# Cross-attention on one core: scores in units that run across tiles, with eight halved slots

## The chip, the cores and the metric

The kernel runs on 1 core of one Trainium2 chip. The metric is the device time of one execution in microseconds (us); the number given for a kernel is the median of its runs.

## The reference

Cross-attention with 16 heads of 32 columns, computed for batch 0 alone. Its result, 512 rows of 512 columns, is added to each of the 32 batches of `x`.

```python
q, k, v = tgt @ Wq.T, memory @ Wk.T, memory @ Wv.T   # then split in 16 heads of 32
scores = einsum('bhqd,bhkd->bhqk', q, k) / sqrt(32)
att = einsum('bhqk,bhkd->bhqd', softmax(scores), v)
return tgt + att[0]          # tgt is x, (32, 512, 512) float32; memory is ctx_1024
```

So the arithmetic is that of one batch, and the traffic is `x` in and out: 2 x 33.6 MB, and 4 MB of weights and context.

## The kernel before, in words

Rows. A row of `x` belongs to a partition p, a half J (0 or 1) and a place r (0 or 1) in it: the rearrangement is `b (j p r) d -> p j b r d`. Tile j of the attention (128 rows) is half j // 2, place j % 2. A *slot* in SBUF holds one half of two batches (1 MiB: 4 KB on a partition for each batch). There are 18 slots and 16 groups of two batches (`GROUPS`), so half 0 of all groups and groups 0 and 1 of half 1 fit; the other 14 groups of half 1 are loaded into slots after their rows of half 0 have been stored. In the first part slots 8 to 17 hold weights and context, raw and turned, and are loaded with `x` once those are dead.

Units of adding. When the attention of heads 0 to 7 of tile 0 is there, `FIRST` adds it to the left half of the columns of the *halved* slots (`HALVED`); `SECOND` adds heads 8 to 15 to their right half, and the whole row to the other slots. `ROW_1` is tile 1, `ROW_2` and `ROW_3` are tiles 2 and 3, in half 1. POOL and DVE share the additions by lists of groups (`POOL_HALVED`, `DVE_HALVED`, `POOL_WHOLE`, `DVE_WHOLE`, `POOL_GROUPS`, `DVE_GROUPS`).

DMA. Everything is issued by SP, on one queue, in an order written out by hand (L234 to L280): weights and loads, FIRST's stores, SECOND's stores, with reloads of the first rows of half 1 (`reload_row(0, g)`, for the groups of `BY_ROWS`) behind them, then ROW_1's stores, each followed by a reload that waits for a store three slots back, then the stores of half 1 (`STORED_BY_ROWS` first, row by row, then `LAST_STORE_ORDER`). Where SP waits for an addition, all that stands behind it in this order waits too. A row of a halved slot's store is 1 KB long, that of a whole row 2 KB, and loads or stores of both rows have 4 KB.

Compute. PE multiplies scores (`scores`: three passes of high and low parts, a head's 32 rows being a quarter of the array), DVE takes each head's negative maximum (`head_max`, L684), ACT the exponential and its sum (`exponent`, L604), PE turns the probabilities (`turn_probs`, L405), ACT copies them out (`copy_transposed`, L612), PE weighs the values of four heads (`weigh_values`, L416), DVE copies that out (`copy_att_t`, L696), PE turns it back (`turn_back`, L428), and DVE multiplies with the inverse sums (`normalize`, L710 and L712). Scores have four PSUM banks, head h in bank h % 4, so a head's scores wait for the exponential four heads back. Between the heads of tile j PE makes tile j + 1's queries (`query_chunk`, L347) and turns them (`turn_queries`); ACT empties both. All engines follow orders written out by hand: `heads(j)` on PE, ACT and DVE for tiles 1 to 3, and explicit lists for tile 0. In `heads` before, a tile's first four heads are scored as a group during the tile before, the other twelve in six pairs (`score_pair`).

Of the kernel before, what the change touches and what calls it, by code (L numbers as in the profile page):

```python
# [12 lines left out]
HEADS = 16  # L13
# [6 lines left out]
def cross_attention_add(nc, x, ctx, wq, wk, wv, out):  # L20
# [12 lines left out]
    PAIR = 2  # L33
    PAIRS = HEADS // PAIR
# [24 lines left out]
    LAST_STORE_ORDER = (6, 7, 8, 1, 2, 3, 4, 5, 0, 9, 10, 11, 12, 13, 14, 15)  # L59

    FIRST_ORDER = (0, 1, 3, 2, 5, 7, 4, 6, 9, 8, 10, 11)
    SECOND_ORDER = (0, 1, 2, 3, 4, 5, 6, 7, 8, 9, 10, 11, 12, 14, 13, 15)
# [5 lines left out]
    with ExitStack() as stack:  # L68
# [47 lines left out]
        stored = [sem(f"stored{g}") for g in range(GROUPS)]  # L116
        ident_ready = sem("ident_ready")
# [47 lines left out]
        def scores_through(j, h):  # L165

            if j == 0:  # L170
                return h // HPG + 1
            return HG + (j - 1) * (PAIRS - 1) + (1 if h < HPG else h // PAIR)

# [19 lines left out]
        def _(sp):  # L193
# [48 lines left out]
            for g in range(1, GROUPS):  # L242
# [17 lines left out]
            for n, g in enumerate(SECOND_ORDER):  # L260
# [55 lines left out]
        def _(pe):  # L316
# [53 lines left out]
            def value_chunk(t, c):  # L370
# [7 lines left out]
                if c == C - 1:  # L378
                    last.then_inc(bank_filled, 1)

# [8 lines left out]
            def score_group(j, g):  # L389
                if j == 0:  # L390
                    emptied(pe, "k_t", g)
                if j * HG + g > 0:
                    pe.wait_ge(exp_ready, j * HEADS + g * HPG)
                scores(j, range(g * HPG, (g + 1) * HPG))

            def score_pair(j, pair):
                pe.wait_ge(exp_ready, j * HEADS + pair * PAIR - PAIR)
                scores(j, range(pair * PAIR, (pair + 1) * PAIR))

# [32 lines left out]
            def heads(j):  # L432
# [4 lines left out]
                score_pair(j, 2)  # L437
# [6 lines left out]
                score_pair(j, 3)  # L444
                turn_probs(j, 4)
                turn_probs(j, 5)
# [3 lines left out]
                score_pair(j, 4)  # L450
                turn_probs(j, 6)
                if more:
                    pe.wait_ge(att_t_ready, j * HG + 1)
                    query_chunk(j + 1, 0)
                turn_probs(j, 7)
                if more:
                    query_chunk(j + 1, 1)
                score_pair(j, 5)
                turn_probs(j, 8)
                if more:  # L460
                    query_chunk(j + 1, 2)
                turn_probs(j, 9)
                if more:
                    query_chunk(j + 1, 3)
                score_pair(j, 6)
# [3 lines left out]
                turn_probs(j, 10)  # L469
                if more:  # L470
                    pe.wait_ge(att_t_ready, j * HG + 2)
                    turn_queries(j + 1)
                turn_probs(j, 11)
                score_pair(j, 7)
# [4 lines left out]
                weigh_values(j, 2)  # L479
                turn_probs(j, 14)  # L480
                turn_probs(j, 15)
                if more:
                    score_group(j + 1, 0)
# [51 lines left out]
            score_group(0, 0)  # L535
# [9 lines left out]
            score_group(0, 1)  # L545
# [44 lines left out]
        def _(act):  # L590
# [24 lines left out]
            def heads(j):  # L615
                for h in range(HEADS):
# [28 lines left out]
            exponent(0, 8)  # L645
            exponent(0, 9)
            copy_transposed(0, 6)
            copy_transposed(0, 7)
            exponent(0, 10)
            empty("q", 1)  # L650
# [3 lines left out]
            copy_transposed(0, 10)  # L654
            empty("q_t", 1)
            exponent(0, 12)
            copy_transposed(0, 11)
            exponent(0, 13)
            copy_transposed(0, 12)
# [9 lines left out]
        def _(dve):  # L669
# [71 lines left out]
            def heads(j, unit, adds):  # L741

                for h in range(HPG, HEADS):
                    if h % HPG == 0 and h >= 2 * HPG:
                        copy_att_t(j, h // HPG - 2)
                    if h == HEADS - 2 and j + 1 < T:
                        empty("q_t", j + 1)  # L750
                    head_max(j, h)
                    if h % HPG == 2 and h > HPG:
                        invert_sums(j, h // HPG - 1)
# [84 lines left out]
```

## Time and profile before

| | |
|---|---|
| median of 3 runs | 188.89 us (188.24 to 189.64) |
| the profiled execution | 189.16 us, of which the span (first to last instruction) is 187.1 |
| busy: PE, DVE, ACT, POOL | 130.9, 100.8, 96.7, 80.3 us |
| DMA | 71.52 MB, on the average 382 GB/s; HBM read 37.75 MB, written 33.55 MB |
| granted TensorE clock | 0.893 on the average: full until the last matmul, half after it |

Busy time is no limit by itself here: an engine's order and its waits decide when a unit's sums exist, and SP's queue decides when they can leave. A stretch of the trace is best read by its GB/s and then by what SP waited for.

### The profile page before, as it was taken

How to read it: one execution, taken by the hardware profiler on the slowest of the kernel's cores; microseconds unless marked ns; L12 is line 12 of the kernel's file. 1: busy time of each engine (PE TensorE's matmuls, PEld its weight loads, DVE VectorE, ACT ScalarE, POOL GpSimd, SP SyncE). 2: the span in 40 equal slices, each digit the busy share in tenths (PEclk: the TensorE clock that was granted, in tenths of full speed). 3: DMA queues.
4: the chain of work that ended last, by engine and by line, in shares of the span. 5: the costliest groups of instructions: out<-in, count | busy, mean ns of one | idle time of the engine just before them, and what ended most of it. 6: DMA issues, size and time to landing. Idle time of an engine off the chain costs nothing.

```text
span 187.1 us, 3330 instructions
## 1 busy us (share of the span) xinstructions
PE 130.9 (70%) x1224; PEld 92.0 (49%) x1224; DVE 100.8 (54%) x161; ACT 96.7 (52%) x225; POOL 80.3 (43%) x43
## 2 busy tenths in 40 slices
PE   6999999999996887998979998889884000000000
PEld 6978857677654665556656556656653000000000
DVE  0263226625517889927399659665453999800000
ACT  2344536378266979777789569698892000000000
POOL 1000000000006959950059999089992999700000
PEclk9999999999999999999999999999999755555555
DMA  6999999999999989999999999999999999999994
GB/s 200 369 384 420 409 408 411 409 409 408 349 404 403 342 294 316 340 299 398 405 387 399 355 401 407 407 403 409 412 416 412 405 421 416 408 421 421 421 421 172
DMA packets 30880, 71.52 MB, mean 382 GB/s; under 512 B 1808, under 2 KB 7952, under 8 KB 30736
## 3 DMA queue, kind: packets, MB, share of 16 engines
q1 hardware_dynamic: 30864, 71.31, 99.7%
q8 instruction: 10, 0.16, 0.3%
q14 instruction: 6, 0.05, 0.1%
HBM read 37.75 MB, written 33.55 MB: 381 GB/s over the span
## 4 chain that ended last, share of the span: by engine, by line
PE 54%; ACT 15%; DVE 11%; issue 6%; DVEq 1%; POOL 0%; ACTq 0%; POOLq 0%
PE bank L405 12%; PE bank L385 8%; ACT probs L604 8%; PE bank L347 8%; PE bank L365 6%; PE bank L376 6%; ACT probs_t L612 5%; PE bank L340 5%; DVE slots L738 5%; PE bank L416 4%; DVE slots L728 3%; PE bank L488 3%; DVE neg_max L684 2%; PE bank L428 1%; DVEq L68 1%
## 5 line engine op out<-in xcount | busy, mean ns | idle before, releaser
L295 POOL TENSOR_TENSOR slots<-slots,att_rows 128x512 f32<-128x512 f32 (+1 forms) x25 | 43.0, 1765 | 72.4 <-DVE att_rows L710 72.4
L604 ACT ACTIVATE probs<-bank,neg_max 128x512 f32<-128x512 f32 x64 | 44.8, 702 | 11.6 <-DVE neg_max L684 11.2
L684 DVE TENSOR_REDUCE neg_max<-bank 128x1 f32<-128x512 f32 x64 | 41.7, 681 | 13.6 <-PE bank L385 13.4
L405 PE MATMUL bank<-ident,probs 128*128 128x128 f32 x256 | 39.8, 281 | 7.7 <-ACT probs L604 6.7
L612 ACT COPY probs_t<-bank 128x512 f32<-128x512 f32 x64 | 37.6, 591 | 11.5 <-PE bank L405 10.5
L405 PEld LDWEIGHTS bank<-ident,probs 128*128 128x128 f32 x256 | 28.1, 141 | 23.3 <-ACT probs L604 17.7
L385 PE MATMUL bank<-k_t,q_t 32*128 32x512 f32 x192 | 24.1, 425 | 0.0
L304 POOL TENSOR_TENSOR slots<-slots,att_rows 128x1024 f32<-128x1024 f32 x8 | 18.6, 2360 | 5.6 <-DVE att_rows L710 5.6
L312 POOL TENSOR_TENSOR slots<-slots,att_rows 128x2048 f32<-128x2048 f32 x4 | 18.0, 4522 | 3.4 <-DVE att_rows L710 3.4
L416 PE MATMUL bank<-probs_t,v 128*32 128x128 f32 x512 | 17.3, 276 | 0.7 <-ACT probs_t L612 0.7
L721 DVE TENSOR_TENSOR slots<-slots,bank 128x512 f32<-128x512 f32 (+1 forms) x19 | 17.5, 930 | 0.1
L347 PE MATMUL bank<-wq_t,att_rows 128*128 128x512 f32 x32 | 16.3, 600 | 0.0
L385 PEld LDWEIGHTS bank<-k_t,q_t 32*128 32x128 f32 x192 | 12.2, 183 | 7.9 <-issue 3.8
L416 PEld LDWEIGHTS bank<-probs_t,v 128*32 128x32 f32 x512 | 13.0, 110 | 5.8 <-issue 2.7
L696 DVE COPY att_t<-bank 128x128 f32<-128x128 f32 x16 | 4.5, 284 | 18.3 <-PE bank L416 18.3
L365 PE MATMUL bank<-ctx_t,wk_t 128*128 128x512 f32 x48 | 13.3, 409 | 0.4 <-ACT ctx_t L598 0.3
L604 ACT ACTIVATION_READ_ACCUMULATOR probs<-bank,neg_max 128x1 f32 x64 | 13.6, 212 | 0.0
L376 PE MATMUL bank<-wv_t,ctx_t 128*128 128x512 f32 x48 | 13.3, 410 | 0.0
L365 PEld LDWEIGHTS bank<-ctx_t,wk_t 128*128 128x128 f32 x48 | 8.3, 189 | 2.3 <-ACT ctx_t L598 0.6
L376 PEld LDWEIGHTS bank<-wv_t,ctx_t 128*128 128x128 f32 x48 | 8.3, 189 | 2.0 <-issue 0.7
L728 DVE TENSOR_TENSOR slots<-slots,bank 128x1024 f32<-128x1024 f32 x8 | 9.1, 1214 | 0.0
L738 DVE TENSOR_TENSOR slots<-slots,bank 128x2048 f32<-128x2048 f32 x4 | 8.9, 2277 | 0.0
(41 smaller groups left out, 91.3 us busy)
## 6 DMA issues: line engine op xcount, KB each, us to landing
slots<-in_x_dram SPq DMA_DIRECT2D x21, 1024.0 KB, 15.6
out_dram<-slots SPq DMA_DIRECT2D x30, 512.0 KB, 9.8
slots<-in_x_dram SPq DMA_DIRECT2D x22, 512.0 KB, 8.9
out_dram<-slots SPq DMA_DIRECT2D x11, 1024.0 KB, 13.5
out_dram<-slots SPq DMA_DIRECT2D x24, 256.0 KB, 3.3
ctx_raw<-in_ctx_dram SPq DMA_DIRECT2D x1, 1024.0 KB, 5.0
wq_raw<-in_L_xattn_Wq_dram SPq DMA_DIRECT2D x1, 1024.0 KB, 9.2
wv_raw<-in_L_xattn_Wv_dram SPq DMA_DIRECT2D x1, 1024.0 KB, 12.1
```

Source lines behind the costliest of these rows:

```text
L295: nc.gpsimd.tensor_tensor(xs, xs, a.unsqueeze(1).to_broadcast([P, BPS, a.shape[1]]), ALU.add).then_inc(added[g], 1)
L304: nc.gpsimd.tensor_tensor(xs, xs, att.unsqueeze(1).to_broadcast([P, BPS, D]), ALU.add).then_inc(row_2_added[g], 1)
L347: last = mm(job_bank("q", j), x0_t[:, c, :], wq_t[:, c, :], start=(c == 0), stop=(c == C - 1))
L365: last = mm(job_bank("k_t", g), wk_t[:, c, a, g * P:(g + 1) * P], ctx_t[:, c, b, :], start=(c == 0 and (a, b) == PASSES[0]), stop=(c == C ...
L376: last = mm(job_bank("v", t), ctx_t[:, c, a, t * P:(t + 1) * P], wv_t[:, c, b, :], start=(c == 0 and (a, b) == PASSES[0]), stop=(c == C - ...
L385: last = mm(bank[:, h % S_BANKS, :], q_t[rows, j % 2, g, a, :], k_t[rows, g, b, :], start=((a, b) == PASSES[0]), stop=((a, b) == PASSES[-1]))
L405: last = nc.tensor.transpose(bank[:, PT_BANK + h % 2, t * P:(t + 1) * P], probs[:, h % 2, t * P:(t + 1) * P], ident[:, :])
L416: last = mm(att_t_ps[i * DK:(i + 1) * DK, g, :], v[:, t, h * DK:(h + 1) * DK], probs_t[:, (j * HEADS + h) % PT_SLOTS, t, :], start=(t == 0 ...
L604: nc.scalar.activation(probs[:, h % 2, :], bank[:, h % S_BANKS, :], ACT.Exp, bias=neg_max[:, h:h + 1], scale=1.0, accum_out=row_sum[:, h:h ...
L612: nc.scalar.copy(probs_t[:, (j * HEADS + h) % PT_SLOTS, :, :], bank[:, PT_BANK + h % 2, :].rearrange("p (t n) -> p t n", t=T)).then_inc(pr ...
L684: nc.vector.tensor_reduce(neg_max[:, h:h + 1], bank[:, h % S_BANKS, :], AX_X, ALU.max, negate=True).then_inc(max_ready, 1)
L738: nc.vector.tensor_tensor(xs, xs, back.unsqueeze(1).to_broadcast([P, BPS, ROWS * D]), ALU.add).then_inc(added[g], 1)
```

## The change

- Tiles 1 to 3 are scored in six *units* of heads (0-2, 3-5, 6-8, 9-11, 12-13, 14-15) instead of a group of four and six pairs. Unit 0 of the next tile is scored before turns 14 and 15 and weighing 3, not between turn 15 and weighing 3.
- DVE takes the maxima of a unit together, and an addition or other work between units (`heads` on DVE). Of the next tile it takes heads 0 to 2 ahead of the tile's end.
- In tile 0, PE weighs heads 0 to 7 and scores heads 12 to 15 earlier; the queries of tile 1 come out later (two after the last scores); ACT and DVE follow in their lists.
- Eight slots are halved instead of twelve; `BY_ROWS` has 7 groups instead of 10, `STORED_BY_ROWS` 3 instead of 5, `ROW_LAG` is 12 instead of 13, and the orders of stores follow.
- Slots 14 and 16, which hold the first halves of `ctx_t` and `wv_t`, are loaded after half of the last value tile's chunks (`half_values_done`), slots 15 and 17 after all of them as before.

```diff
+    UNITS = (range(0, 3), range(3, 6), range(6, 9), range(9, 12), range(12, 14), range(14, 16))
-    HALVED = range(12)
-    POOL_HALVED, DVE_HALVED = (1, 3, 5, 7, 9, 10, 11), (0, 2, 4, 6, 8)
-    POOL_WHOLE, DVE_WHOLE = (13, 15), (12, 14)
+    HALVED = range(8)
+    POOL_HALVED, DVE_HALVED = (1, 3, 5, 7), (0, 2, 4, 6)
+    POOL_WHOLE, DVE_WHOLE = (9, 11, 13, 15), (8, 10, 12, 14)
-    BY_ROWS = range(FRESH, FRESH + 10)
-    ADDED_BY_ROWS, STORED_BY_ROWS = (1, 2, 3, 4, 5, 6, 7, 8), (1, 2, 3, 4, 5)
-    LAST_ROW_DVE_GROUPS = (6, 7, 8, 1, 2, 3, 4, 5)
+    BY_ROWS = range(FRESH, FRESH + 7)
+    ADDED_BY_ROWS, STORED_BY_ROWS = (1, 2, 3, 4, 5, 6, 7, 8), (1, 2, 3)
+    LAST_ROW_DVE_GROUPS = (4, 5, 6, 7, 8, 1, 2, 3)
...
-                if g == CTX_T:
-                    sp.wait_ge(bank_filled, number["v", T - 1] + 1)
-                load(0, g)
-            for g in range(FRESH):
-                load(LAST_HALF, g)
-
-            LAG, ROW_LAG = 3, 13
+                if g < CTX_T:
+                    load(0, g)
+            sp.wait_ge(half_values_done, 1)
+            load(0, CTX_T)
+            load(LAST_HALF, 0)
+            sp.wait_ge(bank_filled, number["v", T - 1] + 1)
+            load(0, CTX_T + 1)
+            load(LAST_HALF, 1)
+
+            LAG, ROW_LAG = 3, 12
...
+            def score_unit(j, u):
+
+                pe.wait_ge(exp_ready, j * HEADS + UNITS[u].stop - S_BANKS)
+                scores(j, UNITS[u])
...
                 turn_probs(j, 13)
                 if more:
                     emptied(pe, "q_t", j + 1)
                 weigh_values(j, 2)
+                if more:
+                    score_unit(j + 1, 0)
                 turn_probs(j, 14)
                 turn_probs(j, 15)
-                if more:
-                    score_group(j + 1, 0)
                 weigh_values(j, 3)
...
-            score_group(0, 2)
-            query_chunk(1, 0)
+            score_group(2)
             emptied(pe, "v", T - 1)
             weigh_values(0, 0)
+            query_chunk(1, 0)
+            turn_probs(0, 8)
             query_chunk(1, 1)
-            turn_probs(0, 8)
-            query_chunk(1, 2)
             turn_probs(0, 9)
-            query_chunk(1, 3)
             weigh_values(0, 1)
             turn_probs(0, 10)
+            score_group(3)
+            turn_probs(0, 11)
+            query_chunk(1, 2)
+            query_chunk(1, 3)
+            turn_probs(0, 12)
             raw_queries_out(1)
             turn_back(0, range(HG // 2))
-            turn_probs(0, 11)
-            score_group(0, 3)
             turn_queries(1)
-            turn_probs(0, 12)
             turn_probs(0, 13)
+            turn_probs(0, 14)
             emptied(pe, "q_t", 1)
+            score_unit(1, 0)
             weigh_values(0, 2)
-            turn_probs(0, 14)
             turn_probs(0, 15)
-            score_group(1, 0)
             weigh_values(0, 3)
...
             copy_transposed(0, 10)
+            copy_transposed(0, 11)
+            exponent(0, 12)
+            exponent(0, 13)
+            empty("q", 1)
+            copy_transposed(0, 12)
             empty("q_t", 1)
...
+                maxima(1)
+                next_add()
+                maxima(2)
+                invert_sums(j, 0)
+                copy_att_t(j, 0)
+                next_add()
+                maxima(3)
+                invert_sums(j, 1)
+                next_add()
+                maxima(4)
+                copy_att_t(j, 1)
+                next_add()
+                maxima(5)
                 if j + 1 < T:
-                    head_max(j + 1, 0)
-                    head_max(j + 1, 1)
-                copy_att_t(j, HG - 1)
+                    empty("q_t", j + 1)
+                invert_sums(j, 2)
+                next_add()
+                copy_att_t(j, 2)
                 if j + 1 < T:
-                    head_max(j + 1, 2)
-                    head_max(j + 1, 3)
+                    for h in UNITS[0]:
+                        head_max(j + 1, h)
+                next_add()
+                invert_sums(j, 3)
+                copy_att_t(j, 3)
...
             normalize(SECOND, slice(HEADS // 2, HEADS))
             add(SECOND, DVE_HALVED[0])
-            head_max(1, 3)
-            add(SECOND, DVE_HALVED[1])
-            heads(1, SECOND, list(DVE_HALVED[2:] + DVE_WHOLE))
+            head_max(1, 2)
+            for g in DVE_HALVED[1:]:
+                add(SECOND, g)
+            heads(1, SECOND, list(DVE_WHOLE))
```

On PE, `heads` has its units between the same turns in the order: turns 0, 1, unit 1, turns 2, 3, unit 2, turn 4, weighing 0, turn 5, query 0, turn 6, query 1, unit 3, turn 7, query 2, turn 8, query 3, unit 4, turn 9, weighing 1, turn 10, unit 5, turn 11, the turned queries, turns 12, 13, weighing 2, the next tile's unit 0, turns 14, 15, weighing 3. On ACT, the raw queries of the next tile are emptied after exponential 9 instead of 10, the turned ones after 12 instead of 11.

## Rows read from the trace of the kernel before

**Rows 1.** The page's slices: DMA share in tenths and GB/s, 40 slices.

```profile
DMA  6999999999999989999999999999999999999994
GB/s 200 369 384 420 409 408 411 409 409 408 349 404 403 342 294 316 340 299 398 405 387 399 355 401 407 407 403 409 412 416 412 405 421 416 408 421 421 421 421 172
```

**Rows 2.** Stretches: busy us of each engine, clock, DMA share, GB/s.

```profile
48.00:52.00 4.00, 4.00 (x53) 2.23 (x51) 3.17 (x6) 1.76 (x5) 0.00 (x0) 1.00 0.94 338
...
68.00:72.00 4.00, 3.08 (x24) 2.21 (x23) 3.97 (x9) 3.52 (x10) 3.35 (x3) 1.00 0.76 253
74.00:80.00 6.00, 5.84 (x60) 3.67 (x60) 5.13 (x9) 4.97 (x14) 6.00 (x5) 1.00 1.02 344
...
81.00:86.00 5.00, 5.00 (x55) 3.05 (x54) 1.67 (x6) 3.46 (x8) 0.97 (x1) 1.00 1.02 315
...
97.70:187.10 89.40, 41.00 (x470) 27.07 (x470) 48.18 (x67) 36.53 (x90) 55.74 (x21) 0.78 1.01 396
...
110.00:130.00 20.00, 18.13 (x234) 12.60 (x230) 13.64 (x26) 16.17 (x41) 14.41 (x7) 1.00 1.05 406
...
164.00:182.00 18.00, 0.00 (x0) 0.00 (x0) 0.00 (x0) 0.00 (x0) 0.00 (x0) 0.50 1.03 422
```

**Rows 3.** SP's issues in time; single stores with time from issue to landing.

```profile
58.83 20.75 SPq L201 DMA_DIRECT2D out_dram<-slots  x26
...
146.34 2.61 SPq L207 DMA_DIRECT2D out_dram<-slots  x3
...
L201 SPq DMA_DIRECT2D out_dram<-slots x1: 373/373/373, 69.7 to 69.7; - x1
...
DMA to landing us min/median/max: 2.5/2.5/2.5
...
L201 SPq DMA_DIRECT2D out_dram<-slots x1: 383/383/383, 97.7 to 97.7; - x1
...
DMA to landing us min/median/max: 5.1/5.1/5.1
```

**Rows 4.** The chain that ended last: start, us on the chain, what.

```profile
34.05 0.90 PE bank L385 x12
...
74.82 1.01 PE bank L416 x32
75.83 0.90 PE bank L385 x6
76.73 0.59 PE bank L405 x4
77.32 0.86 PE bank L347 x2
78.18 0.44 PE bank L405 x4
```

**Rows 5.** ACT in time: start, us, line, operation, idle before it.

```profile
62.50 0.73 ACT L604 ACTIVATE probs<-bank,neg_max 128x512 f32<-128x512 f32 x1
63.08 0.24 ACT L604 ACTIVATION_READ_ACCUMULATOR probs<-bank,neg_max 128x1 f32 x1
63.17 0.62 ACT L612 COPY probs_t<-bank 128x512 f32<-128x512 f32 x1
...
71.01 0.69 ACT L604 ACTIVATE probs<-bank,neg_max 128x512 f32<-128x512 f32 x1
```

**Rows 6.** DVE and POOL in time: maxima and sums.

```profile
49.52 2.48 DVE L684 TENSOR_REDUCE neg_max<-bank 128x1 f32<-128x512 f32 x4 [0.66 <-PE bank L385]
...
68.94 0.69 DVE L721 TENSOR_TENSOR slots<-slots,bank 128x512 f32<-128x512 f32 x1
...
75.30 1.21 DVE L721 TENSOR_TENSOR slots<-slots,bank 128x1024 f32<-128x1024 f32 x1
...
96.44 1.22 DVE L721 TENSOR_TENSOR slots<-slots,bank 128x1024 f32<-128x1024 f32 x1
...
68.65 13.32 POOL L295 TENSOR_TENSOR slots<-slots,att_rows 128x512 f32<-128x512 f32 x9 [2.13 <-DVE att_rows L710]
```

More of the change, by code:

```diff
@@ L171, in scores_through @@
                 return h // HPG + 1
-            return HG + (j - 1) * (PAIRS - 1) + (1 if h < HPG else h // PAIR)
+            return HG + (j - 1) * len(UNITS) + 1 + [h in unit for unit in UNITS].index(True)
         def slot_of(J, g):
@@ L250, in _ @@
                     sp.wait_ge(bank_filled, number["k_t", HG - 1] + 1)
[L251 to L257 removed]
+                if g < CTX_T:
[7 more added lines that the diff above has]
+            LAG, ROW_LAG = 3, 12
             for g in FIRST_ORDER:
                 store(FIRST, g)
[L260 removed]
+            for n, g in enumerate(range(GROUPS)):
                 store(SECOND, g)
@@ L379, in value_chunk @@
                     last.then_inc(bank_filled, 1)
+                if (t, c) == (T - 1, C // 2 - 1):
+                    last.then_inc(half_values_done, 1)
             def scores(j, heads_at_once):
@@ L387, in scores, with score_group @@
                 last.then_inc(scores_ready, 1)
[L389 to L398, printed above, removed]
+            def score_group(g):
+                emptied(pe, "k_t", g)
+                if g > 0:
+                    pe.wait_ge(exp_ready, g * HPG)
+                scores(0, range(g * HPG, (g + 1) * HPG))
+            def score_unit(j, u):
+                pe.wait_ge(exp_ready, j * HEADS + UNITS[u].stop - S_BANKS)
+                scores(j, UNITS[u])
             def turn_probs(j, h):
@@ L454, in heads @@
                     query_chunk(j + 1, 0)
+                turn_probs(j, 6)
+                if more:
+                    query_chunk(j + 1, 1)
+                score_unit(j, 3)
                 turn_probs(j, 7)
                 if more:
-                    query_chunk(j + 1, 1)
-                score_pair(j, 5)
+                    query_chunk(j + 1, 2)
                 turn_probs(j, 8)
                 if more:
-                    query_chunk(j + 1, 2)
+                    query_chunk(j + 1, 3)
+                score_unit(j, 4)
                 turn_probs(j, 9)
-                if more:
-                    query_chunk(j + 1, 3)
-                score_pair(j, 6)
                 if more:
@@ L469, in heads @@
                 turn_probs(j, 10)
+                score_unit(j, 5)
+                turn_probs(j, 11)
                 if more:
@@ L479, in heads @@
                 weigh_values(j, 2)
+                if more:
+                    score_unit(j + 1, 0)
                 turn_probs(j, 14)
                 turn_probs(j, 15)
-                if more:
-                    score_group(j + 1, 0)
                 weigh_values(j, 3)
@@ L741, in heads, with maxima, next_add @@
             def heads(j, unit, adds):
[L746 to L753, printed above, removed]
-                    if adds and (h % 2 == 1 or cols_of(unit, adds[0]) != slice(0, D)):
-                        add(unit, adds.pop(0))
-                copy_att_t(j, HG - 2)
-                invert_sums(j, HG - 1)
+                def maxima(u):
+                    for h in UNITS[u]:
+                        head_max(j, h)
+                def next_add():
+                    if adds:
+                        add(unit, adds.pop(0))
+                maxima(1)
[11 more added lines that the diff above has]
+                maxima(5)
                 if j + 1 < T:
-                    head_max(j + 1, 0)
-                    head_max(j + 1, 1)
-                copy_att_t(j, HG - 1)
+                    empty("q_t", j + 1)
+                invert_sums(j, 2)
+                next_add()
+                copy_att_t(j, 2)
                 if j + 1 < T:
-                    head_max(j + 1, 2)
-                    head_max(j + 1, 3)
+                    for h in UNITS[0]:
[3 more added lines that the diff above has]
+                copy_att_t(j, 3)
             for what, i, _ in JOBS[:number["wv_t", C - 1] + 1]:
@@ L776, in _ @@
             empty("v", 3)
-            for h in range(2 * HPG, 3 * HPG):
-                head_max(0, h)
+            head_max(0, 8)
+            head_max(0, 9)
             invert_sums(0, 0)
             copy_att_t(0, 0)
+            head_max(0, 10)
+            head_max(0, 11)
             invert_sums(0, 1)
             copy_att_t(0, 1)
+            for h in range(3 * HPG, HEADS):
+                head_max(0, h)
             normalize(FIRST, slice(0, HEADS // 2))
             add(FIRST, DVE_HALVED[0])
-            head_max(0, 12)
-            head_max(0, 13)
+            empty("q_t", 1)
             add(FIRST, DVE_HALVED[1])
-            head_max(0, 14)
-            empty("q_t", 1)
-            head_max(0, 15)
-            for g in DVE_HALVED[2:]:
-                add(FIRST, g)
+            add(FIRST, DVE_HALVED[2])
             invert_sums(0, 2)
+            head_max(1, 0)
             copy_att_t(0, 2)
+            add(FIRST, DVE_HALVED[3])
+            head_max(1, 1)
             invert_sums(0, 3)
-            head_max(1, 0)
-            head_max(1, 1)
             copy_att_t(0, 3)
-            head_max(1, 2)
             normalize(SECOND, slice(HEADS // 2, HEADS))
             add(SECOND, DVE_HALVED[0])
-            head_max(1, 3)
-            add(SECOND, DVE_HALVED[1])
-            heads(1, SECOND, list(DVE_HALVED[2:] + DVE_WHOLE))
+            head_max(1, 2)
+            for g in DVE_HALVED[1:]:
+                add(SECOND, g)
+            heads(1, SECOND, list(DVE_WHOLE))
             normalize(ROW_1, before=SECOND)
```

33 lines of the change are left out of this document (11 added, 22 removed).

## Prediction

> **What bounds the kernel now.** I read the page's slices first: the DMA share stands at 9 tenths or more from the second slice to the last but one, with one 8, and GB/s is about 400 except in two hollows [rows 1]. The engines are not like that: from 164 to 182 none of them is busy at all [rows 2], and the span ends at 187.1 with transfers alone. So the kernel is a stream of 71.5 MB on one in-order queue, SP's, and an engine counts only where SP has nothing left to issue.
>
> The stretches give the prices [rows 2]: 406 GB/s in runs of 2 KB (110 to 130), 422 GB/s in runs of 4 KB (164 to 182), 344 GB/s in the 1 KB runs of halved stores (74 to 80). Two stretches lose time because the queue is dry: 48 to 52 (338 GB/s; SP waits for the last values before it loads slots 14 to 17) and 68 to 72 (253 GB/s; the twelve FIRST stores are through, SECOND's first sum comes at 69.6). Then SP's issues [rows 3]: FIRST's stores go out from 58.83, ROW_1's from 97.7. SECOND's first store, issued at 69.7 into a dry queue, landed 2.5 us later; ROW_1's first, issued at 97.7, took 5.1. It is 256 KB larger, 0.6 us at 406 GB/s, so on a dry queue it would have landed after 3.1: 2.0 us of other transfers still lay ahead. ROW_1 today arrives with 2.0 us to spare.
>
> **The change part by part.**
>
> *Traffic.* Total bytes stay. Eight halved slots instead of twelve turn 2.1 MB from 1 KB into 2 KB runs: 6.1 - 5.2 = 0.9 us less. Slots 9 to 11 are no longer reloaded row by row. So SP has 7 row reloads (3.7 MB) instead of 10 to send after SECOND, and after ROW_1's first store 36.2 MB remain instead of 34.6: three row loads fewer (-1.57 MB at 406: -3.9 us), three whole ones more (3.15 MB at 422: +7.5), two slots stored whole instead of in rows (-0.2): **+3.4 us** of work behind ROW_1. As a check, 97.7 to 187.1 at 396 GB/s is 35.4 MB [rows 2]: those 34.6 and 0.8 of backlog, the 2.0 us above.
>
> The Trainium skill ("DMA: Bandwidth & Descriptors", Specifications) puts a core's limit to HBM at about 358 GB/s; by it every such difference would cost about an eighth more (estimate from that page: the 3.4 would be 3.9). The trace runs at 406 to 422 [rows 2] and disagrees; the sum goes by the rows.
>
> *Loads 14 and 16 half a value tile earlier.* That fills the hollow at 48 to 52 (4 us at 338 instead of 406: 0.7 us). It only helps if FIRST follows without a gap.
>
> *Tile 0.* I walk PE, ACT and DVE in their new order with the durations of [rows 4, 5]: weighing 1.0, scores 0.9, turned head 0.44 to 0.59, query pair of matmuls 0.86, exponential 0.67 of ACT's time (0.82 until its sum is read), copy 0.6 until done (ACT goes on 0.47 after its start), maximum 0.60 apart [rows 6], under 0.1 for each hand-over. The start is the third score group, the same in both (its maxima begin at 49.52 [rows 6], PE is free at 49.4). Weighing 0, queries 0 and 1 around turn 8, turn 9 at 52.75 (after copy 7), weighing 1 to 54.35, turn 10, scores of 12 to 15 at 54.9, turn 11, queries 2 and 3 to 58.05. ACT now takes exponentials 12 and 13 ahead of the raw queries, which it empties at 58.35 to 58.95; the turn back waits for them, and so FIRST is multiplied at 59.4 and its first sum done at 60.9. **FIRST's first store goes out at 60.95 instead of 58.83.** The wait that caused it is the one for the raw queries; behind it on PE stand the turned queries and turns 13 and 14. Then: turned queries 59.25, exponential 14 at 60.4, turn 14 at 61.25, unit 0 of tile 1 at 61.85, weighing 2 at 62.75, turn 15 at 63.75, copies 14 and 15, weighing 3 at 65.15, copied out at 66.3, turned back 66.65, multiplied 67.1, SECOND's first sum from 67.9 instead of 68.94: **1.0 earlier**.
>
> *Tile 1.* PE loses one of seven score stages: pairs and groups of four both take 0.90 [rows 4], so units of three are costed at 0.90 too (bounds 0.90 and 1.35, by heads; nearest to both rows). That is 0.9 us less PE work. But DVE now runs SECOND's sum 0, the maximum of head 2 and three more sums (0.6 each) before the maximum of head 3, which comes at 70.9; exponential 3 starts at 71.6, against 71.01 [rows 5]. Unit 2 needs exponential 4 (73.6), weighing 0 is at 75.1, its copy on DVE behind three maxima at 76.5, the first query at 76.85. From there PE has 11.2 us without a gap to 88.0 (four queries, units 3 to 5, turns 6 to 12, weighing 1, turned queries). It then waits for exponential 13, which stands on ACT behind the turned queries' copy, till 89.1. Turn 13, weighing 2, next tile's unit 0, turns 14 and 15 follow; weighing 3 must wait for copy 15, which the next tile's scores no longer cover, till 93.5. Copied out 94.65, turned back 95.0, multiplied 95.7, ROW_1's first sum from 97.0 instead of 96.44 [rows 6]. What the units save on PE goes into these two waits. **ROW_1's first store: 98.25 instead of 97.7.**
>
> *SECOND's whole sums.* DVE's slots 8, 10, 12, 14 now each follow a unit's maxima. Number 12 follows unit 3 (scored 79.05, maxima to 81.9): done 83.1 instead of 76.5 [rows 6]. POOL's nine sums now take 13.3, to 82.0 [rows 6]; three halved ones go and two whole ones come, each worth about two halved, and it starts a microsecond earlier: done at 81 to 83 again, and slot 13 is in time. SP issues in slot order, so behind slot 12's store stand three more stores and seven reloads.
>
> **The sum.** The queue after FIRST: loads end at 60 to 61, dry till 62.8 (60.95 and 1.85, the 2.5 of [rows 3] less its 0.65 of transfer), eight stores of 0.76 to 68.9, dry till 70.4, SECOND's first twelve slots to about 82, dry till 85.0 when slot 12 comes (83.15 and 1.85), then eleven transfers of 1.29: 99.2, or 100.3 with the 1.1 us that the turn from stores to loads costs now (81 to 86 at 315 GB/s [rows 2]). ROW_1's first store adds 1.85 to 98.25: 100.1. So two gates, the late sum and the late ROW_1, close at the same time. ROW_1's store lands at 98.25 + 3.1 = 101.4 on a dry queue, against 102.8 now: -1.4. Work behind it: +3.4. Slot 2's sum waits for three maxima of tile 2 (about 101.1) and leaves 0.4 dry. Sum **+2.4 us**: 189.16 + 2.4 = 191.6 for the profiled execution, 188.89 + 2.4 = **191.3** for the median. The 2.1 us between execution and span stay. Costs bounded from both sides: units at 1.35 add up to 2.3 us in tile 1 (five units) before PE's waits take some; the hand-overs, 0 to 0.1 for some thirty steps, are worth 1.5 either way; so 189.8 to 193.6 for this case alone. The last tile is no gate: from 100.1 the queue has 18.5 MiB of ROW_1's stores and reloads and three row stores ahead of the first whole slot, to about 152; now that slot's store goes out at 146.34 [rows 3], so tiles 2 and 3 would have to take 3 us longer than today to be late.
>
> **The rivals.**
> (a) *Faster: the queue never dries behind FIRST.* If SECOND's sum 0 were ready by 67 and slot 12 and ROW_1 kept ahead, the stream alone would count: 62.8 + 6.1 (FIRST) + 6.1 and 10.3 (SECOND's halves and whole rows) + 9.0 (seven reloads) + 1.1 (the turn) = 95.4 for ROW_1, 4.7 before the forecast: 186.6. It decides if ROW_1's first store is issued before 93.7, 4 us earlier than now. For it: one score stage less. Against it: PE's waits are for ACT. Chance 0.13.
> (b) *No change: the units do shorten tile 1 by 2 to 3 us* (exponential 13 and copy 15 not waited for: 1.1 + 0.9, and sum 12 as much earlier). ROW_1's stream begins at 97 to 98: 188.3 to 189.5. For it: ACT and PE both stand idle at those two places, so a small shift in order closes them. Chance 0.26.
> (c) *The added sums between units hold up ROW_1's and SECOND's stores as well*, a dry microsecond at each of slots 4, 6 and 8: 194 to 195. Chance 0.07.
> (d) *The forecast:* 0.54.
>
> **How the numbers follow.** One per cent, 1.9 us, is what a measurement here can tell from no change. Range 187.2 to 193.8: it leaves out (a) and (c), 0.2 together. Faster by over 1% (under 187.0): 0.11 of (a) and 0.03 of (b)'s lower edge, 0.14. Slower by over 1% (over 190.8): most of (d), 0.46, and all of (c), 0.07, together 0.53. Within: 0.33.
>
> **What would show it.** Right: FIRST's first store near 61, hollows in GB/s near 61 and 83, ROW_1's first store after 97 and landing about 3 us later, slot 12's sum after 82. Wrong: ROW_1's first store before 95 with transfers queued ahead of it, or PE without gaps after turn 12. A unit of three that takes over 1.0 would be a price of mine that fell.

## The result, and the profile after

The changed kernel takes 193.55 us (median of four runs, 193.23 to 193.69) beside 188.56 us of the kernel before in the same runs (188.03 to 189.64): ratio 1.0255, 95% interval 1.0204 to 1.0305. It is slower, as forecast, and inside the range; the size is +5.0 us where +2.4 was forecast. The profiled execution took 193.44 us, its span 191.7, so 1.7 lies outside it (2.1 before). Ratios here and below leave out executions more than 1.5% above the fastest of the same kernel (among them two of four in e3 and in e4, four of ten in e8 and in e10; the profiles of e3 and e8 are of such executions and are not used), so a ratio can differ from that of two medians.

The page's slices of after (TensorE clock in tenths, DMA share in tenths, GB/s; a slice is 4.8 us):

```profile
PEclk9999999999999996999999999999999855555555
DMA  6999999999997979649999999999999999999995
GB/s 214 365 373 421 408 409 409 409 409 410 410 405 283 337 253 362 242 150 355 403 399 361 282 401 400 404 417 418 410 412 419 407 421 421 412 419 420 423 421 233
```

The hollow of before in slice 11 [rows 1] is filled, and new ones stand in slices 13, 15, 17 and 18: 283, 253, 242, 150. The clock's line has a 6 at slice 16, which before had nowhere until its last matmul. The stretches of after say when and why (busy us of each engine, clock, DMA share, GB/s):

```profile
46.85:58.00 11.15, 10.69 (x122) 6.40 (x120) 6.29 (x13) 7.83 (x20) 0.00 (x0) 1.00 1.03 409
60.00:62.00 2.00, 1.82 (x25) 1.26 (x29) 2.00 (x5) 1.28 (x5) 2.00 (x3) 1.00 0.65 229
66.00:68.00 2.00, 2.00 (x20) 1.43 (x19) 1.97 (x5) 0.58 (x1) 1.53 (x2) 1.00 0.56 187
73.00:76.00 3.00, 3.00 (x34) 1.93 (x34) 1.97 (x4) 1.73 (x5) 3.00 (x2) 0.50 1.04 362
78.00:80.00 2.00, 2.00 (x16) 1.08 (x14) 0.06 (x1) 1.72 (x5) 2.00 (x2) 1.00 0.51 187
82.00:84.00 2.00, 2.00 (x11) 0.82 (x10) 1.44 (x3) 1.69 (x5) 0.00 (x0) 1.00 0.04 11
84.00:86.00 2.00, 2.00 (x40) 1.55 (x40) 1.66 (x4) 1.63 (x5) 0.00 (x0) 1.00 0.84 261
86.00:88.00 2.00, 2.00 (x17) 1.51 (x16) 1.96 (x3) 1.59 (x4) 0.00 (x0) 1.00 0.99 275
88.00:98.00 10.00, 7.89 (x114) 5.79 (x113) 5.68 (x12) 7.73 (x20) 1.24 (x1) 1.00 1.05 400
98.57:191.70 93.13, 39.30 (x472) 26.20 (x470) 48.93 (x68) 37.60 (x91) 55.71 (x21) 0.78 1.01 395
150.00:186.00 36.00, 0.00 (x0) 0.00 (x0) 16.49 (x11) 0.00 (x0) 15.99 (x4) 0.52 1.03 418
```

A low GB/s with a share near 1 is slow transfers; a low share is a queue with nothing to send, called dry here. A *gate* is a store that SP cannot issue before its sum exists, while all that stands behind it in SP's order waits too. At 82 to 84 the share is 0.04, and SP waits for slot 12's sum. SP's issues, its waits for these sums of DVE (37.7 us in 13 waits, the longest 12.1; before, 20.0 us in 8), and ROW_1's first store from issue to landing:

```profile
59.93 23.91 SPq L198 DMA_DIRECT2D out_dram<-slots  x21
...
98.57 3.84 SPq L198 DMA_DIRECT2D out_dram<-slots  x4
...
SPq L198 <- DVE slots L723: 37.7, 13, 12.1
...
L198 SPq DMA_DIRECT2D out_dram<-slots x1: 384/384/384, 98.6 to 98.6; - x1
...
DMA to landing us min/median/max: 5.2/5.2/5.2
```

ROW_1's first store was issued at 98.57, 0.9 later than before [rows 3], and landed at 98.57 + 5.2 = 103.8. The sum turned on this number: 101.4 was forecast, 102.8 was before. From it to the span's end are 191.7 - 103.8 = 87.9 us, against 187.1 - 102.8 = 84.3 before: +3.6, where +3.4 was forecast.

PE in time (start, us, line, operation, idle before it and its cause), then DVE:

```profile
71.31 0.66 PE L408 MATMUL bank<-ident,probs 128*128 128x128 f32 x4 [1.73 <-ACT probs L606]
72.47 1.29 PE L387 MATMUL bank<-k_t,q_t 32*128 32x512 f32 x9 [0.50 <-ACT probs L606]
73.68 1.12 PE L408 MATMUL bank<-ident,probs 128*128 128x128 f32 x4
74.73 1.84 PE L419 MATMUL bank<-probs_t,v 128*32 128x128 f32 x32
...
79.34 0.97 PE L387 MATMUL bank<-k_t,q_t 32*128 32x512 f32 x9
...
84.48 1.08 PE L419 MATMUL bank<-probs_t,v 128*32 128x128 f32 x32
...
89.48 0.66 PE L408 MATMUL bank<-ident,probs 128*128 128x128 f32 x4 [0.97 <-ACT probs L606]
...
93.80 1.08 PE L419 MATMUL bank<-probs_t,v 128*32 128x128 f32 x32 [0.73 <-ACT probs_t L614]
```

```profile
58.42 0.42 DVE L712 TENSOR_TENSOR att_rows<-bank,recip 128x256 f32<-128x256 f32 x1 [1.04 <-PE bank L431]
...
66.77 0.69 DVE L723 TENSOR_TENSOR slots<-slots,bank 128x512 f32<-128x512 f32 x1
...
82.25 1.19 DVE L723 TENSOR_TENSOR slots<-slots,bank 128x1024 f32<-128x1024 f32 x1
...
95.99 0.69 DVE L712 TENSOR_TENSOR att_rows<-bank,recip 128x512 f32<-128x512 f32 x1 [0.75 <-PE bank L431]
...
97.32 1.22 DVE L723 TENSOR_TENSOR slots<-slots,bank 128x1024 f32<-128x1024 f32 x1
...
123.50 0.69 DVE L712 TENSOR_TENSOR att_rows<-bank,recip 128x512 f32<-128x512 f32 x1 [0.75 <-PE bank L431]
...
147.23 0.69 DVE L712 TENSOR_TENSOR att_rows<-bank,recip 128x512 f32<-128x512 f32 x1 [0.75 <-PE bank L431]
```

Nine matmuls are a unit of three: 0.97 to its last end, 0.90 to the start of the next (79.34, then 80.25), the price forecast; the two waits for ACT (0.97 and 0.73) are the forecast's 1.1 and 0.9. Not forecast is the half clock from 73 to 76, after PE had idled 1.73: there a unit takes 1.29 and a weighing 1.84 instead of 1.08.

### The profile page after: what moved, and what is told of

Its sections match the earlier page's. It is cut to its first block and busy times, and to the rows that moved or that the text cites. A ratio compares the mean times of both kernels' runs of the same rounds, so it can differ in the third digit from the quotient of the medians.

```text
span 191.7 us, 3318 instructions
## 1 busy us (share of the span) xinstructions
PE 128.3 (67%) x1224; PEld 90.6 (47%) x1224; DVE 102.5 (53%) x161; ACT 97.4 (51%) x225; POOL 77.4 (40%) x39
## 5 line engine op out<-in xcount | busy, mean ns | idle before, releaser
L295 POOL TENSOR_TENSOR slots<-slots,att_rows 128x1024 f32<-128x1024 f32 (+1 forms) x21 | 40.1, 1945 | 76.1 <-DVE att_rows L712 76.1
L686 DVE TENSOR_REDUCE neg_max<-bank 128x1 f32<-128x512 f32 x64 | 40.5, 684 | 19.4 <-PE bank L387 19.3
L387 PE MATMUL bank<-k_t,q_t 32*128 32x512 f32 x192 | 21.6, 431 | 3.3 <-ACT probs L606 3.3
L419 PE MATMUL bank<-probs_t,v 128*32 128x128 f32 x512 | 18.1, 284 | 2.8 <-ACT probs_t L614 2.8
L723 DVE TENSOR_TENSOR slots<-slots,bank 128x1024 f32<-128x1024 f32 (+1 forms) x19 | 18.5, 984 | 0.1
L419 PEld LDWEIGHTS bank<-probs_t,v 128*32 128x32 f32 x512 | 13.6, 113 | 6.4 <-ACT probs_t L614 3.9
L387 PEld LDWEIGHTS bank<-k_t,q_t 32*128 32x128 f32 x192 | 10.8, 183 | 10.9 <-ACT probs L606 6.5
```

The lines of the kernel that those rows point to most:

```text
L295: nc.gpsimd.tensor_tensor(xs, xs, a.unsqueeze(1).to_broadcast([P, BPS, a.shape[1]]), ALU.add).then_inc(added[g], 1)
L387: last = mm(bank[:, h % S_BANKS, :], q_t[rows, j % 2, g, a, :], k_t[rows, g, b, :], start=((a, b) == PASSES[0]), stop=((a, b) == PASSES[-1]))
L419: last = mm(att_t_ps[i * DK:(i + 1) * DK, g, :], v[:, t, h * DK:(h + 1) * DK], probs_t[:, (j * HEADS + h) % PT_SLOTS, t, :], start=(t == 0 ...
L686: nc.vector.tensor_reduce(neg_max[:, h:h + 1], bank[:, h % S_BANKS, :], AX_X, ALU.max, negate=True).then_inc(max_ready, 1)
L723: nc.vector.tensor_tensor(xs, xs, a.unsqueeze(1).to_broadcast([P, BPS, a.shape[1]]), ALU.add).then_inc(added[g], 1)
```

## The experiments

Two theories stood at first. Q: the queue decides, by the time that it is dry ahead of ROW_1's stores and the work that is left behind them. R: the work behind ROW_1 alone (three groups fewer by rows) is the loss. Where an expectation names another rival, the run's reading says what it is.

**e1: ten groups by rows again.** Diff against after:

```diff
-    BY_ROWS = range(FRESH, FRESH + 7)
+    BY_ROWS = range(FRESH, FRESH + 10)
```

> The changed kernel with 10 groups in BY_ROWS again instead of 7 and nothing else: three more row loads go out between SECOND's stores and ROW_1's, and 3.4 us less work is left behind ROW_1. Theory Q (two gates on one queue: slot 12's late sum, with everything behind it, binds first): the three loads stand behind slot 12 in either place, so no change, 193.0 to 194.0. Rival R (what counts is how much is left behind ROW_1): 3.4 us faster, 190.1. Rival C (tile 1's arithmetic is slower, the queue only follows): no change.

Measured 193.85 us, ratio 1.0254 (1.0163 to 1.0345). No gain; R falls. The work behind ROW_1's store did shrink, to 84.15 us, but the store itself was issued at 99.25 and landed 8.7 later:

```profile
L198 SPq DMA_DIRECT2D out_dram<-slots x1: 383/383/383, 99.2 to 99.2; - x1
...
DMA to landing us min/median/max: 8.7/8.7/8.7
```

```profile
82.00:84.00 2.00, 2.00 (x10) 0.93 (x9) 2.00 (x4) 1.69 (x5) 0.00 (x0) 1.00 0.04 8
```

The three added row reloads stood behind slot 12's store, and the dry stretch ahead of that stayed. So bytes moved from behind one gate to in front of it shortened nothing here, where they filled no dry stretch.

**e2: reloads from the tenth store on,** ahead of the late sum.

```diff
-            LAG, ROW_LAG = 3, 12
+            LAG, ROW_LAG = 3, 9
```

> The changed kernel with ROW_LAG 9 instead of 12: the seven row loads go out behind SECOND's stores of slots 9 to 15, so three of them lie ahead of the wait for slot 12's sum and fill the dry stretches at 78 to 80 and 82 to 85. Q: the first gate opens 2.6 to 3.9 us earlier, then ROW_1's own first store (issued 98.6, 1.85 to the first byte, against 101.7 now) binds: 1.0 to 1.5 us faster, 192.0 to 192.5. R: no change, the bytes behind ROW_1 are the same. C: no change.

Measured 194.88 us, 1.0287 (1.0224 to 1.0351), no gain where Q had 1 to 1.5. Stretches:

```profile
78.00:88.00 10.00, 10.00 (x83) 6.02 (x85) 6.69 (x11) 7.26 (x17) 3.64 (x2) 0.98 0.96 322
88.00:90.00 2.00, 1.98 (x18) 1.37 (x14) 1.80 (x3) 1.77 (x5) 0.00 (x0) 1.00 0.87 145
98.00:102.00 4.00, 2.74 (x24) 1.82 (x22) 3.97 (x7) 3.57 (x9) 3.78 (x2) 1.00 0.44 163
```

The hollow at 78 to 88 is mostly filled, and the queue is dry at 98 to 102 instead, for ROW_1 (issued at 100.03, landed 2.8 later). Two gates stood one behind the other. This profile also has half a clock from 72 to 78, 3.4 us longer than after, and ROW_1's store goes out 1.5 later; the execution whose mean clock was nearest to after's (0.887, after 0.886) took 193.32, no gain that shows either.

**e3: both,** `BY_ROWS` of ten and `ROW_LAG` 8.

> Both edits, 10 groups in BY_ROWS and ROW_LAG 8. Q: the gate of slot 12 opens and 3.4 us of work leave the place behind ROW_1, so the gains no longer hide each other: 1.3 + 3.4 = 4.7 us faster, 188.5 to 189.5, though the two alone give 0 and 1.3. R: 3.4 faster, 190.1, as with the ten groups alone. C: no change.

Measured 1.013 (1.0062 to 1.0197), from two of four executions (191.56 and 191.62; the others took 194.82 and 195.12). In these two both edits together give some 2 us of the 4.7 expected, where neither gave anything alone; the interval overlaps that of e1, so this is a sign and not settled.

**e4: DVE takes each of the maxima 3, 4, 5 of tile 1 ahead of one of SECOND's halved sums** (`first=2` leaves that unit out of `heads`).

```diff
...
-            for g in DVE_HALVED[1:]:
+            for h, g in zip(UNITS[1], DVE_HALVED[1:]):
+                head_max(1, h)
                 add(SECOND, g)
-            heads(1, SECOND, list(DVE_WHOLE))
+            heads(1, SECOND, list(DVE_WHOLE), first=2)
```

> The changed kernel with DVE's order at the start of tile 1 changed: maxima of heads 3, 4, 5 each ahead of one of SECOND's sums 2, 4, 6 instead of behind all three; all on SP as in the changed kernel. Exponential 3 should start about 0.8 us earlier (69.7 instead of 70.5), and if the granted clock no longer falls at 72.5 to 76.5 another 1.5 us come back. Q: slot 12's sum and ROW_1 move together, 0.8 to 2.3 us faster, 191.2 to 192.7. R: no change. C: the same 0.8 to 2.3, so this run tells only R from the others and shows whether the clock's fall hangs on PE's idle time before turn 3.

Ratio 1.0157 (1.0084 to 1.023), from two of four executions, 191.74 and 192.47, in the range of Q and C; the others took 196.09 and 197.03. In the profiled one, 191.74, PE's idle time before turn 3 fell from 1.73 to 0.98, the clock stayed full, ROW_1's first store landed at 97.24 + 4.9 = 102.1. By this DVE's order at that place is worth about 1% (1.0255 less 1.0157), but the two intervals overlap, and the same edit gains nothing that shows in e10.

**e5: PE kept busy in that gap** by twelve turns of the identity into an unused bank, which change no result.

```diff
                 turn_probs(j, 2)
+                if j == 1:
+                    pe.wait_ge(probs_t_ready, j * HEADS + 2)
+                    for _ in range(12):
+                        nc.tensor.transpose(bank[:, PT_BANK + 1, 0:P], ident[:, :], ident[:, :])
                 turn_probs(j, 3)
```

> The changed kernel with twelve transposes of the identity (overwritten by the next turn) between turns 2 and 3 of tile 1, where PE otherwise idles for 1.73 us; nothing else is moved. Theory K (the fall of the granted clock behind that idle time costs what tile 1 loses): the clock stays at full through 72 to 76, slot 12's sum and ROW_1 come 1.2 to 1.5 us earlier, 192.0 to 192.5 against 193.5. Rival S (the clock falls for another reason, or the stretch at half the clock is hidden): no change in the clock or none in the time, 193.2 to 193.8.

Measured 193.62 us, 1.0234 (1.0199 to 1.0269): no gain that shows, in the range of S. Its stretches:

```profile
72.00:76.00 4.00, 3.50 (x53) 2.25 (x50) 3.29 (x8) 3.22 (x9) 4.00 (x2) 1.00 1.02 353
...
100.00:105.00 5.00, 4.76 (x50) 3.46 (x51) 3.31 (x7) 2.68 (x9) 5.00 (x3) 0.66 1.01 363
```

The clock held at 72 to 76, slot 12's sum came 22.53 us behind FIRST's multiplication (58.80 to 81.33) instead of 23.83 (58.42 to 82.25), and ROW_1's store landed at 102.1, as in e4. Then the clock fell in tile 2, after 1.27 of idle, and once more at 128, and 89.3 us lay behind that store instead of 87.9. So K had the clock and the sums right and the time wrong. The fall at 73 is worth 1.3 us at ROW_1; that it costs the kernel that much is not shown: of e5's four executions the one with the highest mean clock, 0.893, took 193.79, the two with the lowest, 0.880, 193.23 and 193.45.

**e6: the change's compute with the slots of before** (twelve halved, ten by rows, `ROW_LAG` 13 and the store orders of before). **e7: the reverse,** compute of before with the change's slots and loads as before. The lines of the slots are those of the diff of the change.

> All of the changed kernel's order of compute on PE, ACT and DVE, with the slots, shares and store orders of the kernel before (twelve halved, ten reloaded by rows). Q (the queue: eight halved slots put 3.4 us behind ROW_1 and leave two dry stretches in SECOND): most of the loss goes, only ROW_1 comes about 1 us later than before, 189.5 to 190.5. C (the loss is in the new order of compute): stays at 193 to 194.

> The kernel before, its order of compute untouched, with the changed kernel's slots (eight halved, seven reloaded by rows, lag 12, store orders). Q: FIRST's eight stores end at 67, dry until SECOND at 71.4, ROW_1's store on an almost empty queue at 99.5 and 3.4 us more behind it: 191.0 to 192.0. C: as the kernel before, 188.5 to 189.3.

e6 192.02 us, 1.0151 (1.0092 to 1.0209); e7 191.77 us, 1.0134 (1.0098 to 1.0171). e7 is in Q's range; e6 is over Q's and under C's, so both rivals missed there. Each half of the change costs by itself, and their sum, 1.0285, is about the whole, 1.0255. In e7 the stretches that SECOND's and slot 10's sums leave dry:

```profile
66.00:70.00 4.00, 3.26 (x25) 2.40 (x24) 3.97 (x9) 3.52 (x10) 2.44 (x2) 1.00 0.15 50
...
78.00:80.00 2.00, 2.00 (x10) 0.91 (x10) 1.65 (x2) 1.97 (x5) 2.00 (x2) 1.00 0.29 103
```

FIRST now has eight stores instead of twelve, four times 0.76 us less to send before SECOND is there; the whole sums that took the place come later than halved ones did.

**e8: e1, e4 and `ROW_LAG` 8 together.**

> The changed kernel with ten groups by rows, lag 8 and the maxima of heads 3 to 5 each ahead of one of SECOND's sums. Q: slot 12 is no gate, 3.4 us less stand behind ROW_1, and ROW_1's first store goes out at about 97.2 as in the run with the maxima first: 188 to 189, the kernel before within a per cent. C: only the maxima's gain, 191.5.

Ten executions, median 192.23 (189.86 to 194.56); the ratio, 1.0082 (1.0037 to 1.0127), is that of the faster six. 188 to 189 was expected, and the best four were at 189.86 to 190.02. In those most of the loss is taken back; a gain over before was not reached.

**e9: tile 0's new order and the split loads alone,** with pairs, `heads` and slots of before. **e11: the split loads alone,** added to before.

```diff
-                if g == CTX_T:
-                    sp.wait_ge(bank_filled, number["v", T - 1] + 1)
-                load(0, g)
-            for g in range(FRESH):
-                load(LAST_HALF, g)
+                if g < CTX_T:
+                    load(0, g)
+            sp.wait_ge(half_values_done, 1)
+            load(0, CTX_T)
+            load(LAST_HALF, 0)
+            sp.wait_ge(bank_filled, number["v", T - 1] + 1)
+            load(0, CTX_T + 1)
+            load(LAST_HALF, 1)
...
```

> Tile 0's new order and the split loads of the change alone: tiles 1 to 3 with the group and six pairs of the kernel before, twelve halved slots and its store orders. Q (the queue; what moves is when SECOND and ROW_1 reach it): SECOND about 2 us earlier, FIRST's twelve stores run into it without a dry stretch, tile 1 as long as before, so ROW_1's first store goes out about 1.5 us earlier and still meets a backlog; the two hollows of before close: 0.8 to 1.5 us faster than before, 187.5 to 188.3. Rival T (tile 0's order is what costs, since FIRST comes 2 us later): 1 to 2 us slower than before.

> The kernel before with slots 14 and 16 loaded after half of the last value tile's chunks, and nothing else. The hollow at 48 to 52 closes. Q: FIRST's first store then finds the queue almost empty and the dry time before SECOND grows by what was won; ROW_1 still meets a smaller backlog: 0 to 0.5 us faster, 188.6 to 189.2 beside 189.2. Rival L (loads set the pace): 0.7 faster.

e9 189.86 us (median of twelve), 1.0058 (1.0024 to 1.0091): slower by a little, where Q had it faster, though ROW_1 is earlier. Its multiplications of ROW_1 to ROW_3, SP's issues and a stretch:

```profile
93.28 0.68 DVE L717 TENSOR_TENSOR att_rows<-bank,recip 128x512 f32<-128x512 f32 x1
...
119.86 0.68 DVE L717 TENSOR_TENSOR att_rows<-bank,recip 128x512 f32<-128x512 f32 x1
...
141.88 0.69 DVE L717 TENSOR_TENSOR att_rows<-bank,recip 128x512 f32<-128x512 f32 x1 [0.75 <-PE bank L435]
```

```profile
60.85 20.79 SPq L203 DMA_DIRECT2D out_dram<-slots  x26
...
95.85 3.28 SPq L203 DMA_DIRECT2D out_dram<-slots  x4
```

```profile
60.00:62.00 2.00, 1.08 (x18) 0.74 (x20) 1.97 (x5) 2.00 (x6) 2.00 (x2) 1.00 0.20 74
```

ROW_1's store is issued at 95.85 and lands 8.1 later, at 104.0: the queue, not ROW_1, holds it. FIRST's first store, at 60.85 as the forecast had it (60.95), found that queue dry: at 74 instead of 408 GB/s the stretch 60 to 62 loses 1.6 us, about what the kernel lost (1.1 by the ratio). So T, that FIRST's delay costs by itself, is borne out. e11 measured 188.74 us, 1.0017 (0.9989 to 1.0045): filling the hollow at 48 to 52 alone gains nothing that shows.

**e10: e6 with e4's order of maxima.**

> The changed kernel's compute with the slots of the kernel before (as the run with twelve halved), and the maxima of heads 3 to 5 each ahead of one of SECOND's sums. Q, with the start of tile 1 as the place where the new order loses: PE's idle time before turn 3 falls from 2.3 us to about 1.0, ROW_1's first store from 99.9 to 97.5, and the time to that of before within 1 us, 188.5 to 189.8. U (the units themselves lengthen tile 1): stays near 192.

Ten executions, median 192.02 (190.10 to 193.50), 1.0124 (1.0082 to 1.0166) by the faster six; 188.5 to 189.8 was expected, and it is not told apart from e6, whose interval overlaps.

**e12: before with split loads, fourteen halved slots and twelve groups by rows,** the slots moved the other way.

```diff
-    HALVED = range(12)
-    POOL_HALVED, DVE_HALVED = (1, 3, 5, 7, 9, 10, 11), (0, 2, 4, 6, 8)
-    POOL_WHOLE, DVE_WHOLE = (13, 15), (12, 14)
+    HALVED = range(14)
+    POOL_HALVED, DVE_HALVED = (1, 3, 5, 7, 9, 10, 11, 13), (0, 2, 4, 6, 8, 12)
+    POOL_WHOLE, DVE_WHOLE = (15,), (14,)
...
-    BY_ROWS = range(FRESH, FRESH + 10)
+    BY_ROWS = range(FRESH, FRESH + 12)
...
```

> The kernel before with the split loads, fourteen halved slots instead of twelve and twelve groups reloaded by rows instead of ten: the opposite direction of the change. Q: two more FIRST stores (1.5 us) fill the dry time before SECOND, at a price of 0.46 us for four more 1 KB stores in place of two 2 KB ones, and two more row loads stand ahead of ROW_1's first store instead of behind it: 0.4 to 1.0 us faster than before, 187.5 to 188.1 beside 188.5. Rival N (1 KB stores cost what the dry time cost): no change. R, by which only the bytes behind ROW_1's first store count (1 MiB fewer, 2.6 us): 186.

Measured 188.26 us beside 189.12, 0.9977 (0.9943 to 1.0011): not told apart from before, and 186 is excluded. Work behind ROW_1's store is down to 80.7 us (landed at 97.5 + 7.5 = 105.0 of 185.7), and the store lands 2.2 later than in before: what left the one side stands on the other, as in e1. No version here beats before by more than its interval.

## Why the prediction was right, and short by half

**Direction and mechanism: right.** FIRST's store later, a hollow at 61 and one at 83, slot 12's sum after 82, ROW_1's store after 97: all came. Against the forecast: FIRST's store 59.93 for 60.95 and SECOND's sum 66.77 for 67.9 (all of this program ran about 1.2 us earlier from its start on: the third score group's maxima began at 48.30, 49.52 before, in code that is the same), slot 12's sum done 83.4 for 83.1, ROW_1's issue 98.57 for 98.25. From SECOND's first sum to ROW_1's, tile 1 took 30.55 us (66.77 to 97.32), 27.5 before [rows 6] and 29.1 forecast. The half clock at 73 to 76 is nearly all of the difference to the forecast: e5, whose clock held in tile 1, took 29.24 (67.15 to 96.39). It ate the earlier start, so that ROW_1's issue came within 0.4 of the forecast is luck.

**The step that failed: "ROW_1's store lands at 98.25 + 3.1 = 101.4 on a dry queue, against 102.8 now: -1.4".** It landed at 103.8, +1.0; the work behind it came to +3.6 for +3.4, and the 0.4 for slot 2 needed no place of its own. 1.0 + 3.6 = 4.6, the difference of the spans. But a transfer has 16 completions in the trace, one for each DMA engine, and a landing is the last of them. In after 14 of the 16 parts of this store landed 2.7 to 3.0 us after the issue, one 3.4 and one 5.2; the 16 parts of slot 12's store, issued into a dry queue at 83.47, took 2.8 to 3.1. So for nearly all of the queue the store landed at 101.3 to 101.6, as forecast, and the two gates did "close at the same time": of the eleven transfers from slot 12's store on (5.77 MB) 5.07 MB had moved by 98 (the stretches from 84 to 98 above), and the rest, at 400 GB/s, is through at 99.8, for 99.2 to 100.3. The late part was already 2.3 us behind the other 15 at slot 15's store (issued at 88.10, 9.3 us for 6.6 to 7.0); what held it, no run shows.

What failed is the number on the other side of the subtraction, "102.8 now" with "2.0 us of other transfers" ahead of ROW_1. Before, the parts of that store took 3.1 to 5.1 us, half of them at most 3.5: most of the 2.0 was the lag of a few engines and not a queue. By the median part of each, ROW_1's store came at 101.4 for 101.1, +0.3 where -1.4 was forecast, and 90.3 us lay behind it for 86.0, +4.3 where 3.4 and slot 2's 0.4 were. Of the 2.2 us between 2.4 and 4.6 this term is 1.7 and the work behind 0.5. The 1.85 us in the sum were read wrongly too: on a dry queue the first packet started 0.9 us after the issue (67.48, 78.09 and 83.47), and the rest of the 1.85 comes after the data.

**The work behind ROW_1.** Over the kernels it follows the groups by rows: 80.7 us with twelve (e12), 83.4 to 85.7 with ten (before, e1, e6, e9, e10, e11), 87.0 to 90.6 with seven (after, e2, e4, e5, e7); from the median part's landing 82.3, 85.2 to 86.3, and 88.6 to 90.8. So the price of the term holds roughly. As a cause it is half a truth, since e1 took the term away and gained nothing. What the time follows is how much the queue moved before that. The stretch that holds all the gates is 58 to 112; here in before, after and e2:

```profile
58.00:112.00 54.00, 48.17 (x522) 31.20 (x521) 40.10 (x73) 41.80 (x101) 37.96 (x23) 1.00 1.02 359
```

```profile
58.00:112.00 54.00, 45.20 (x476) 29.45 (x480) 38.83 (x69) 38.93 (x94) 34.43 (x19) 0.97 0.90 314
```

```profile
58.00:112.00 54.00, 45.29 (x467) 29.64 (x467) 38.26 (x68) 38.71 (x94) 32.99 (x18) 0.94 0.89 306
```

After moved 45 GB/s x 54 us = 2.43 MB less there, 6.0 us at 408 GB/s; it had moved 23 GB/s x 12 us more from 46 to 58 (408, before 385), 0.7 us. Left: 5.3 us late, and the span is 4.6 longer. The same reckoning for each profile:

| kernel | GB/s, 58 to 112 | late by it | span less 187.1 |
|---|---|---|---|
| e11 | 360 | -0.8 | -0.6 |
| e12 | 358 | -0.5 | -1.4 |
| e9 | 347 | +0.9 | +1.0 |
| e10 | 341 | +1.7 | +1.2 |
| e6 | 336 | +2.4 | +1.7 |
| e4 | 327 | +3.6 | +2.8 |
| e7 | 321 | +4.4 | +3.0 |
| e1 | 316 | +5.0 | +5.0 |
| after | 314 | +5.3 | +4.6 |
| e5 | 314 | +5.3 | +4.3 |
| e2 | 306 | +6.3 | +6.3 |

Eleven profiles agree within 1.4 us; each is a single execution, and before's own spans run from 185.0 to 188.1. The table is bookkeeping: it tells where the time is lost, not why. The lost time is the queue's loss between FIRST and ROW_1; the last 70 us give nothing back, all kernels running there at 400 to 420 GB/s.

**Who dries the queue.** By parts: tile 0's order +0.6% (e9 against e11's nothing), the units about +0.9% on top (e6 against e9, 1.0151 and 1.0058; the intervals almost meet), the slots +1.3% alone (e7). The units were to save PE 0.9 us in a tile, and the forecast let two waits for ACT eat it. They eat more: from ROW_1's to ROW_2's multiplication a tile takes 27.51 us in after (95.99 to 123.50) and 26.58 with pairs (e9, 93.28 to 119.86), the next 23.73 and 22.02, with after's clock full between 96 and 123. PE's longer waits for ACT in the first of these tiles, in after and then in e9:

```profile
100.01 0.66 PE L408 MATMUL bank<-ident,probs 128*128 128x128 f32 x4 [1.25 <-ACT probs L606]
...
116.86 0.66 PE L408 MATMUL bank<-ident,probs 128*128 128x128 f32 x4 [0.97 <-ACT probs L606]
...
121.17 1.08 PE L419 MATMUL bank<-probs_t,v 128*32 128x128 f32 x32 [0.73 <-ACT probs_t L614]
```

```profile
96.59 0.66 PE L412 MATMUL bank<-ident,probs 128*128 128x128 f32 x4 [0.92 <-ACT probs L611]
...
113.34 0.66 PE L412 MATMUL bank<-ident,probs 128*128 128x128 f32 x4 [0.50 <-ACT probs L611]
```

With one more in each (0.50 in after, 0.18 in e9) they are 3.45 us for 1.60: 1.85 more, less the 0.9 saved, is the 0.93 measured. Rival (b) fell on that. Rival (c), sums that hold up stores, had its dry microseconds at slots 4, 6 and 8, where SP's stores show none; but slot 10's sum, which stands between units too, leaves one (78 to 80 at 187 GB/s) that the forecast had not.

**The chances.** Slower had 0.53, more than the other two, and within 1% 0.33. By their ratios, within 1% stayed only kernels with pairs and at least twelve halved slots (e9, e11, e12), and e8, with its three further edits.

The Trainium skill's limit of 358 GB/s, which the prediction set against the rows, is in "Perfetto Trace Analysis" (Roofline) a share that one core alone may exceed, up to about 435. The trace agrees with that: 418 from 150 to 186. The work behind ROW_1, +3.6 by the last part and +4.3 by the median part, does not decide between the 3.4 by the rows and the 3.9 by the Trainium skill.

**Open.** Why 0.5 to 1.4 us of the table's lateness don't show in the span of seven of the eleven kernels (all but e1, e2, e9 and e11); the rate of the last stores varies from 403 to 419 GB/s between the profiles (150 to 180), worth more than a microsecond, and that was not controlled. How much of the 2.5% is the clock's fall: e5 moved it, and no profile was without one in all tiles and else the same. Why one DMA engine falls 2 us behind the others, and whether that costs the end anything: no run tests it.

## What to carry to other kernels

With one in-order queue, list every gate in order with the time at which the bytes ahead of it are through. Do not read a backlog from the time between a store's issue and its landing: that is the time of its slowest DMA engine, 2.4 us behind the middle one in after and 1.6 before. Then count the bytes that the queue moves over the stretch that holds all the gates: an edit that shifts bytes from behind a gate to in front of it, or fills one hollow, gains only if the sum of the dry time falls. An engine's stages merged to save work may give it all back, and more, in waits for the engine between.

## What the runs showed of the hardware that was not expected

The granted TensorE clock fell to half in the middle of the work, 2.4 to 1.2 GHz, for 3 to 7 us. With 1.73 us of idle before turn 3 (after, e1, e2) it fell each time, and after 2.33 (e6); after 0.98 and 0.99 (e4, e10) it stayed full there. But e7 fell at 73 to 77 with a gap of 0.92 that before and e9 have too without a fall, and 1.35 at 61 in before was followed by none. In tile 2 a gap of 1.27 was followed by a fall in e5 and one of 1.25 in e1 (102 to 105), the same 1.25 in after by none. So a gap is not enough to tell, and what else decides stayed open. The same work took 1.84 us for 1.08 meanwhile (a weighing).

The 16 parts of one transfer landed within 0.3 us of each other after a dry stretch (slot 12's store in after, ROW_1's in e2), but 2.5 us apart in ROW_1's store in after (2.7 to 5.2) and 2.0 in before (3.1 to 5.1), where transfers had run for some 14 us without a dry stretch, with one or a few engines behind the rest.
